# A gated recurrence over 512 steps: three groups of the input projection ahead of the candidate's product, and GpSimd's subtraction of x between its two other operations

## The reference

```python
vz, vr, vh = cond @ C_z + b_z, cond @ C_r + b_r, cond @ C + b
xz, xr, xh = x @ W_z, x @ W_r, x @ W          # for all 512 steps
def step(h, t):
    z = sigmoid(xz[t] + h @ U_z + vz)
    r = sigmoid(xr[t] + h @ U_r + vr)
    hh = tanh(xh[t] + (r * h) @ U + vh)
    return (1 - z) * h + z * hh
# h starts at zero; the result is x + all the h
```

## Time and profile before

| what | value |
|---|---|
| median of 3 runs | 2455.28 us (2454.91 to 2456.19) |
| the profiled execution | 2454.7 us, of which 2452.5 us lie between its first and last instruction (its span) |
| PE busy | 2334.5 us (95% of the span) |
| DVE busy | 1864.7 us (76%) |
| ACT busy | 1045.2 us (43%) |
| POOL busy | 629.8 us (26%) |
| granted clock of TensorE, mean | 0.994 of full speed |

### The profile page before, as it was taken

How to read it: one execution, slowest core, us unless ns; L and a number is a source line. 1 busy time by engine, 2 the same in 40 slices (tenths; PEclk the granted TensorE clock), 3 DMA queues, 4 the chain that set the end, 5 groups by cost and what they waited for, 6 DMA issues and landing times.

```text
span 2452.5 us, 186249 instructions
## 1 busy us (share of the span) xinstructions
PE 2334.5 (95%) x83078; PEld 1921.6 (78%) x83078; DVE 1864.7 (76%) x7717; ACT 1045.2 (43%) x3091; POOL 629.8 (26%) x1165
## 2 busy tenths in 40 slices
PE   1999999999999999999999999999999999999998
PEld 1788887888788887888878888788887888878887
DVE  3777777777777777777777777777777777777776
ACT  1444444444444444444444444444444444444443
POOL 0222222222222222222222222222222222222222
PEclk8999999999999999999999999999999999999999
DMA  9101101101101101101111011011011011011000
GB/s 187 25 18 35 35 18 35 35 18 35 35 18 35 35 18 35 30 22 35 26 26 35 18 34 35 18 35 35 17 35 35 18 35 35 18 35 35 18 18 20
DMA packets 145362, 78.17 MB, mean 32 GB/s; under 512 B 9024, under 2 KB 140608, under 8 KB 145216
## 3 DMA queue, kind: packets, MB, share of 16 engines
q1 hardware_dynamic: 145216, 76.84, 13.1%
HBM read 43.25 MB, written 33.55 MB: 31 GB/s over the span
## 4 chain that ended last, share of the span: by engine, by line
PE 87%; DVE 9%; issue 1%; SPq 1%; ACT 1%; DMA 1%; ACTq 0%; POOLq 0%; POOL 0%; DVEq 0%
PE p_bank L231 40%; PE banks L223 34%; PE banks L253 12%; DVE h_lo L503 6%; DVE banks L424 2%; DMA w_stage<-in_L_cond_W_r_dram 1%; SPq L135 0%; ACT L352 0%; SPq L130 0%; PE p_bank L239 0%; DVE w_lo L446 0%; DVE w_top L432 0%; SPq L141 0%; ACT L350 0%; ACT gate_r L352 0%
## 5 line engine op out<-in xcount | busy, mean ns | idle before, releaser
L231 PE MATMUL p_bank<-w_hi,x_t 128*32 128x384 f16 x16384 | 1101.4, 327 | 5.7 <-DVE w_lo L446 5.7
L231 PE MATMUL p_bank<-w_lo,x_t 128*32 128x384 f16 x8192 | 704.0, 326 | 0.0
L231 PEld LDWEIGHTS p_bank<-w_hi,x_t 128*32 128x32 f16 x16384 | 467.4, 97 | 129.7 <-issue 6.0
L223 PE MATMUL banks<-u,reset_t 128*32 128x128 f32 x16384 | 551.0, 275 | 7.3 <-DVE reset_t L517 6.0
L223 PE MATMUL banks<-u,h_t 128*32 128x128 f32 x16384 | 540.0, 273 | 2.9 <-DVE h_t L533 2.9
L223 PEld LDWEIGHTS banks<-u,reset_t 128*32 128x32 f32 x16384 | 417.5, 109 | 151.9 <-DVE reset_t L517 129.4
L424 DVE SCALAR_TENSOR_TENSOR banks<-p_bank,x_down,base 128x128 f32<-128x128 f32 x1536 | 478.6, 342 | 47.3 <-PE p_bank L231 9.2
L223 PEld LDWEIGHTS banks<-u,h_t 128*32 128x32 f32 x16384 | 465.9, 110 | 45.8 <-DVE h_t L533 1.9
L202 POOL TENSOR_TENSOR result<-x_nat,state 128x128 f32<-128x128 f32 x512 | 234.2, 457 | 910.0 <-DVE state L531 910.0
L196 POOL TENSOR_TENSOR kept<-keep,state 128x128 f32<-128x128 f32 x512 | 234.5, 458 | 893.5 <-ACT keep L354 893.5
L515 DVE TENSOR_TENSOR reset<-gate_r,state 128x64 f32<-128x64 f32 x1024 | 208.6, 204 | 188.4 <-ACT gate_r L352 188.3
(11 more groups left out here) (55 smaller groups left out, 1884.9 us busy)
## 6 DMA issues: line engine op xcount, KB each, us to landing
x_nat<-in_x_dram SPq DMA_DIRECT2D x256, 128.0 KB, 3.1
out_dram<-result SPq DMA_DIRECT2D x256, 128.0 KB, 2.7
c_w<-in_L_cond_C_r_dram SPq DMA_DIRECT2D x4, 256.0 KB, 7.5
c_w<-in_L_cond_C_z_dram SPq DMA_DIRECT2D x4, 256.0 KB, 10.6
c_w<-in_L_cond_C_dram SPq DMA_DIRECT2D x4, 256.0 KB, 13.7
u<-in_L_cond_U_z_dram SPq DMA_DIRECT2D x4, 256.0 KB, 16.6
w_stage<-in_L_cond_W_r_dram SPq DMA_DIRECT2D x4, 256.0 KB, 17.9
w_stage<-in_L_cond_W_z_dram SPq DMA_DIRECT2D x4, 256.0 KB, 17.7
```

The source lines that it names most:

```text
L223: last = nc.tensor.matmul(out[part(j)], turned[:, part(q)], weights[:, q, cols(j)], start=first and q == 0, stop=q == Q - 1, skip_group_ch ...
L231: last = nc.tensor.matmul(p_bank[k][part(j), 0:G * N], x_t[:, c, part(q), a], w[b][:, :, q, cols(j)], start=f == 0, stop=f == GROUPS - 1, ...
```

## The change

Two things change. First, `BEFORE_C` goes from 2 to 3: one more group of four projection matmuls stands ahead of C in every step, and one fewer behind it. Second, GpSimd's subtraction stands between `kept` and `result` of the step with t = 0 and no longer behind `result`. To have its input ready there, the three preparations on ACT come one step earlier: the sum at t = 1, `x_whole` at t = 2, and the high part at t = 3 of the set before, so that one more high part (of set 1) is made ahead of the loop. DVE's instructions are the same in the same order, as are SP's.

```diff
-    BEFORE_C = 2
+    BEFORE_C = 3
...
-    SUM_STEP, WHOLE_STEP, HIGH_STEP, TURN_AHEAD = 2, 3, 0, 3
+    SUM_STEP, WHOLE_STEP, HIGH_STEP, LOW_STEP, TURN_AHEAD = 1, 2, 3, 0, 3
...
                 nc.gpsimd.tensor_tensor(kept[:], keep[:], state[:, (tt - 1) % SLOTS], ALU.mult).then_inc(kept_ready, 1)
 
+                if tt % SET == LOW_STEP and not (last and m == STEPS // SET):
+                    sets = i * (STEPS // SET) + (m + 1)
+                    rest_of_x(m % 2, sets if first or last else pool.snap(sets))
+
                 o = j % OUTS
...
                 nc.gpsimd.tensor_tensor(result[o][:, t], x_nat[j % BUFS][:, t], state[:, tt % SLOTS], ALU.add)\
                     .then_inc(out_ready, 1)
-                if tt % SET == HIGH_STEP and not (last and m == STEPS // SET):
-                    sets = i * (STEPS // SET) + (m + 1)
-                    rest_of_x(m % 2, sets if first or last else pool.snap(sets))
...
             whole_x(1)
+            high_x(1)
...
-                if t == HIGH_STEP and more(1):
-                    act.wait_ge(x_t_ready, count(SET * now_m + TURN_AHEAD))
-                    high_x(m + 1)
+                if t == HIGH_STEP and more(2):
+                    act.wait_ge(x_t_ready, count(SET * (now_m + 1)))
+                    high_x(m + 2)
```

## The result

The changed kernel takes 2372.95 us (median of 4 runs, 2371.08 to 2373.72), against 2455.72 for the kernel before on the same chip (median of 4 runs too). The ratio is 0.966, with a 95% interval of 0.965 to 0.968: 82.8 us less. Forecast were 2374, in a range of 2362 to 2405.

The account below looks back on a forecast made before the run. TensorE was taken as the bound, with standing still at C and `h_lo`. Per set 0.53 + 0.33 - 0.24, with rounding, gave 0.64 us; times 127, 81 us less: 2374 us, range 2362 to 2405.

Parts of the forecast that it names:

- Where the time was lost: TensorE's standing still per four-step set: 0.33 us at C, 0.53 at the update's last third, waiting for `h_lo`.
- The ordinary step of 4.38, where the two limits meet: TensorE's work and the path over `h_t` both give R + 4.38 us; an ordinary step took 4.52 before.
- The late loads: Loads of C and R released close to their products; a load that late costs its product 0.02 us.
- the 0.02 of the sum: Extra 0.02 us for a late load, counted in the path from C to the next R, C + 2.34.
- the rival with unhidden loads: Products need their loads' full 0.16 us lead; set 18.74, 2491 us, slower than before; chance 0.04.
- `taken` held to R + 4.07: In t = 0 the subtraction shuts out `taken`, which ends 0.24 us late; that step takes 4.68.
- that rival: The transposition of x on DVE is shut out too, `taken` 0.47 us late: 2403 us; chance 0.08.
- the rival of a delayed subtraction: DVE's queued seeds and transposition keep the subtraction out until R + 3.04; `taken` 0.64 us late: 2425 us; chance 0.04.
- that of a free `taken`: `taken` is not shut out by the subtraction; t = 0 takes 4.44 us: 2344 us; chance 0.05.
- The sum: A four-step set takes 17.82 us instead of 18.46, 0.64 less; times 127 gives 81 us.
- 127 waits for `h_t`: Expected in the changed kernel's table of waits, where there were few before.
- few for `reset_t`: Expected in the changed kernel's table of waits, which had 390 such waits before, three in each set.

Follow-up runs that it names:

- The halves with two groups: Changed kernel with the subtraction split in two, behind `kept` in t = 0 and t = 1, and BEFORE_C = 2: 2407.69 us, ratio 0.981 against the kernel before.
- the halves: Changed kernel (three groups) with GpSimd's subtraction split into two 128x256 parts, behind `kept` in t = 0 and t = 1: 2343.73 us, ratio 0.955 against the kernel before.
- the third group alone: Kernel before with BEFORE_C = 3 and nothing else; expected about 2409 us, 46 us less; measured 2428.76 us, ratio 0.989.

## Why the prediction was right

- *Where the time was lost* (0.33 a set at C, 0.53 at `h_lo`): confirmed apart from each other. The halves with two groups remove the second alone, and a hole of 0.13 at C comes back in t = 1: 0.53 - 0.13 = 0.40 a set would be 51 us, and 47 were measured. The third group on top removes the holes, now four of 0.13, 0.13, 0.13 and 0.07: 0.46 x 128 = 59, and 63 were measured. The steps themselves go from 4.52 to 4.38 three times and to 4.43 once, 0.51 a set and 65 us; the 0.05 beyond the holes fits the 0.02 that a late load of C costs, but was not measured apart.
- *The ordinary step of 4.38, where the two limits meet*: 4.37 and 4.38 measured. That 4.38 is a limit from both sides is shown by four groups, which cost 61 us, and by two, which cost 63 with the halves. The path over `h_t` is 2.32 from C to R by the run with four groups, so with C at R + 2.04 it would allow 4.36; TensorE's own work needs the 4.38, and 0.02 are to spare.
- *The late loads*: R begins 0.02 behind its load and the step has lost nothing that the starts show. In the step after the real wait, t = 1, the load and R start together and the step takes 4.39. So the 0.02 of the sum was due only there, and the rival with unhidden loads, from a needed lead of 0.11 (0.12 by its own terms), is out: a lead of 0.02 to 0.04 did.
- *`taken` held to R + 4.07*: 1203.75 less 1199.68 is 4.07. The step takes 4.66 against 4.68 forecast, and TensorE waits 0.23 against 0.24. `taken` is held in 121 of the 127 sets; in the other six, each the first of a block of the loop, C comes so late that `taken` is issued behind the subtraction. The transposition of x kept its 0.30 inside the subtraction, so that rival is out as well; the rival of a delayed subtraction is out by its start at R + 2.64; and that of a free `taken` by its 0.54.
- *The sum*: 0.66 in the set shown against 0.64 forecast, 82.8 us against 81. The spans of the two profiled executions differ by 81.5 us (2452.5 and 2371.0), 0.64 for each of 127 sets.
- *What it had wrong*: "127 waits for `h_t`" and "few for `reset_t`" in the table of waits. There are 502 and 397, since a load that is issued early and waits 0.18 counts there, though its product is in time. What lies outside the 128 sets was put down to the start, but that is 72 of the 92 us; most of the rest is the end and the longer first step of each block (6.19 and not 4.52 before), which the change leaves as they are. And it wrote the two parts down as if each had its price alone. The sum was right since it was made for both together, with the times of `taken` taken from the later C; the two edits priced singly, in the expectation for the third group alone, missed by 20 us.

## What to carry to other kernels

Fill work moved ahead of a waiting product is free until the recurrence behind it loses its own cover; work out the path on both sides, and stop where the two meet. Here that was 4.38 us on both, one group further costs 61 us. A reserve on the recurrence may be paying for another wait somewhere else, so edits have to be priced together (26 and 28 us singly, 83 together). And where GpSimd works beside a recurrence on VectorE, look at which VectorE instructions with two SBUF inputs can be issued while it runs: shorten GpSimd's instruction to end before them, or keep one of their inputs in PSUM. These took another 28 and 31 us here.

## What the runs showed of the hardware

- A DVE instruction with two inputs in SBUF that is issued during a GpSimd tensor_tensor on SBUF ends 0.14 to 0.15 us after it (`h_lo`, `taken`, 128x128), and the 128x64 ones (`state`, `reset`) 0.08. One with an input in PSUM, or a transposition with one input, is not held: 287 ns and 0.30 us.
- The hold is lifted when the GpSimd instruction that was running ends, also if the next one follows: `taken` got in between two subtractions 0.07 us apart, and `reset` between `kept` and a half that follow each other at once. One issued during the second subtraction is held by that (`state`, 1.25 us).
- Halving a GpSimd subtraction of 128x512 (1.28 us) gave 0.73 us for 128x256, so some 0.18 of each, an estimate (2 x 0.73 less 1.28), is not proportional to its size.
- A product whose load was released 0.02 to 0.04 us ahead of it was not late, where the usual lead in this kernel is 0.16.
